# Attention and expert sums on one core: two banks for the weighted sums, other periods for the normalisation pieces, one rounding moved to VectorE

## The reference

```python
xn = _layernorm(x, axis=-1)
Q = einsum('bnd,hdk->bhnk', xn, proj_q); K = einsum('bmd,dk->bmk', xn, proj_k); V = einsum('bmd,dv->bmv', xn, proj_v)
weights = softmax(einsum('bhnk,bmk->bhnm', Q, K), axis=-1)
Y = einsum('bhnv,hdv->bnd', einsum('bhnm,bmv->bhnv', weights, V), proj_o)
mid = einsum('amh,ehn->aemn', xn, w1); ffn = einsum('aemn,enh->amh', mid, w2)
return x + Y + ffn
```

## Time and profile before

| what | us |
|---|---|
| median of 3 runs | 1715.02 |
| the runs | 1715.01, 1715.02, 1720.04 |
| the profiled execution | 1721.89 |
| its span | 1720.1 |
| PE busy | 1664.0 (97%) |
| POOL busy | 1334.9 (78%) |
| ACT busy | 1293.4 (75%) |
| DVE busy | 1280.9 (74%) |

### The profile page before, as it was taken

One profiled execution on the slowest core, in us unless ns is written; L12 is line 12 of the kernel. 1 busy time (PEld: TensorE's weight loads), 2 busy tenths in 40 slices (PEclk: granted clock), 3 DMA queues, 4 the chain that ended last, 5 costly groups with the idle time before them and its releaser, 6 DMA issues. The chain is left out here.

```text
span 1720.1 us, 46064 instructions
## 1 busy us (share of the span) xinstructions
PE 1664.0 (97%) x18808; PEld 1220.2 (71%) x18808; DVE 1280.9 (74%) x2754; ACT 1293.4 (75%) x1294; POOL 1334.9 (78%) x955
## 2 busy tenths in 40 slices
PE   6689999999999999999999999999999999999997
PEld 5567777777777777777777777777777777777774
DVE  4467777777777777777777777777777777777774
ACT  3467777777777777777777777777777777777774
POOL 0377887887887887888878878878878878788786
PEclk8899999999999999999999999999999999999999
DMA  7000000000000000000000000000000000000000
GB/s 223 1 2 2 2 2 8 8 2 2 2 13 3 2 2 2 14 2 2 2 8 8 2 2 2 8 8 2 2 2 8 8 2 2 2 14 2 2 2 13
DMA packets 16142, 16.70 MB, mean 10 GB/s; under 512 B 384, under 2 KB 12160, under 8 KB 15936
## 3 DMA queue, kind: packets, MB, share of 16 engines
q1 hardware_dynamic: 13856, 12.72, 2.5%
q10 hardware_dynamic: 2080, 1.05, 0.2%
HBM read 9.57 MB, written 4.19 MB: 8 GB/s over the span
## 5 line engine op out<-in xcount | busy, mean ns | idle before, releaser
L252 POOL TENSOR_TENSOR pr_lo<-pr,pr_hi 128x1024 f16<-128x1024 f32 x512 | 1087.6, 2135 | 338.8 <-ACT pr_hi L333 331.7
L326 ACT ACTIVATE pr<-s_ps,boost,scale 128x1024 f32<-128x1024 f32 x512 | 617.0, 1205 | 258.9 <-PE s_ps L457 240.9
L634 DVE TENSOR_REDUCE key_max<-s_ps 128x128 f16<-128x1024 f32 x512 | 625.9, 1223 | 0.5
L333 ACT ACTIVATE pr_hi<-pr 128x1024 f16<-128x1024 f32 x512 | 525.4, 1051 | 8.1
L455 PE MATMUL s_ps<-g_lo,xT 128*128 128x128 f16 x4096 | 516.1, 220 | 2.2 <-DVE g_lo L647 0.9
L457 PE MATMUL s_ps<-g_hi,xT 128*128 128x128 f16 x4096 | 515.6, 220 | 0.0
L455 PEld LDWEIGHTS s_ps<-g_lo,xT 128*128 128x128 f16 x4096 | 401.0, 98 | 42.3 <-DVE g_lo L647 10.1
L457 PEld LDWEIGHTS s_ps<-g_hi,xT 128*128 128x128 f16 x4096 | 402.5, 98 | 30.4 <-issue 0.6
L363 PE MATMUL t_ps<-pr_hi,xn_hi 128*128 128x512 f16 x1024 | 389.3, 380 | 21.0 <-POOL pr_lo L252 7.3
L365 PE MATMUL t_ps<-pr_hi,xn_lo 128*128 128x512 f16 x1024 | 389.2, 380 | 0.0
L364 PE MATMUL t_ps<-pr_lo,xn_hi 128*128 128x512 f16 x1024 | 389.2, 380 | 0.0
(11 more groups left out here) (108 smaller groups left out, 1548.8 us busy)
## 6 DMA issues: line engine op xcount, KB each, us to landing
out_dram<-xacc SPq DMA_DIRECT2D x16, 256.0 KB, 2.3
w_sb<-in_L_ffn_w_dram SPq DMA_DIRECT2D x1, 2048.0 KB, 12.9
xacc<-in_L_attn_x_dram SPq DMA_DIRECT2D x1, 640.0 KB, 7.9
pr<-in_L_attn_proj_q_dram ACTq DMA_DIRECT2D x1, 512.0 KB, 4.6
pr<-in_L_attn_proj_o_dram ACTq DMA_DIRECT2D x1, 512.0 KB, 6.8
wkv<-in_L_attn_proj_k_dram SPq DMA_DIRECT2D x1, 64.0 KB, 2.8
wkv<-in_L_attn_proj_v_dram SPq DMA_DIRECT2D x1, 64.0 KB, 4.4
w_sb<-in_L_ffn_w_dram SPq DMA_DIRECT2D x1, 0.5 KB, 19.1
```

Source lines behind the costliest of these rows:

```text
L252: pool.tensor_tensor(pr_lo[:, u % RING, :], pr32[:, u % PR, :], pr_hi[:, u % RING, :], ALU.subtract)\
L326: act.activation(pr32[:, u % PR, :], both_banks(u), ACT.Exp, bias=boost[:, 0:1], scale=scale[:, 0:1])\
L333: act.activation(pr_hi[:, u % RING, :], pr32[:, u % PR, :], ACT.Copy).then_inc(p_hi_ready, 1)
L634: dve.tensor_reduce(key_max[:, u % 2, :], both_banks(u).rearrange("p (t q) -> p q t", q=P), AX_X, ALU.max).then_inc(keys_max, 1)
```

## The change

- `t_ps` has two banks; block k sums into bank k mod 2 (`sum_bank`), and `turn_ps` is gone. The maxima are turned, and put into a row, in the bank that is idle; where n mod 4 = 2 they are turned in a half bank of the next unit's scores, whose second high pass therefore waits for `max_found`.
- Tile 0 of a block's sum moves from n mod 4 = 3 to the period before: its first product goes ahead of the turn of the maxima, the two others behind it. Every period then has two tiles. It waits for `p_lo_ready` 4k + 4 as before, for `t_lo_ready` k - 1 instead of k, and for a `bias_ready` that the low passes just before it wait for too.
- In n mod 4 = 3 the row of maxima is made right behind the second high pass, and `place_bias` stands ahead of `max_of_keys` as in the other periods.
- Normalisation pieces: `bn_stats` from n mod 8 = 2 to 0, `bn_aggr` from 3 to 1, epsilon from 6 to 3, `rstd` on GpSimd from 7 to 4, `normalise` from the next pair's 2 to the same pair's 7, `split_high` from 3 to 4, `xn_lo` on GpSimd from 4 to 5.
- The last unit's `pr_lo` and the last addition of head outputs go to VectorE.

```diff
-        t_ps = pb("t_ps", [P, BANK])
-        turn_ps = pb("turn_ps", [P, BANK])
+        t_ps = pb("t_ps", [P, 2 * BANK])
+        turn16 = t_ps[:, BANK:2 * BANK].bitcast(F16)
...
+        def sum_bank(k):
+            return t_ps[:, (k % 2) * BANK:(k % 2 + 1) * BANK]
+        def turn_bank(n):
+            return sum_bank(summing(n) + 1)
+        def maxima_turned(u):
+            if u % 4 == 2:
+                return bank(u + 1, 1)[:, 0:P // 2].bitcast(F16)
+            return turn_bank(u)[:, 0:P // 2].bitcast(F16)
...
-                if n % 8 == 7 and (tile := ln_tile(n // 8)) is not None:
+                if n % 8 == 4 and (tile := ln_tile(n // 8)) is not None:
                     pool.wait_ge(ln_var, tile - AHEAD + 2)
                     pool.tensor_tensor(rstd ...
-                if n % 8 == 4 and (tile := ln_tile(n // 8 - 1)) is not None:
+                if n % 8 == 5 and (tile := ln_tile(n // 8 - 1)) is not None:
                     pool.wait_ge(ln_hi, tile + 1)
                     pool.tensor_tensor(xn_lo ...
-                if 1 <= n <= UNITS:
+                if 1 <= n < UNITS:
                     p_low(n - 1)
...  (high_pass, half 1)
+                    if j == 3:
+                        pe.wait_ge(max_found, u)
...  (weigh)
-                if t == 0:
-                    pe.wait_ge(p_lo_ready, 4 * k + 4)
-                    if k == 0: pe.wait_ge(f_copied, 1)
-                    else: pe.wait_ge(t_lo_ready, k)
+                if first:
+                    if t == 0:
+                        pe.wait_ge(p_lo_ready, 4 * k + 4)
+                        if k >= 2:
+                            pe.wait_ge(t_lo_ready, k - 1)
+                        pe.wait_ge(bias_ready, min(4 * k + 6, UNITS))
+                        if k == 1:
+                            pe.wait_ge(f_copied, 1)
+                    pe.matmul(dst, xn_hi[:, tile, :], p_hi, start=t == 0, stop=False)
+                if rest:
+                    pe.matmul(dst, xn_hi[:, tile, :], p_lo, start=False, stop=False)
+                    done = pe.matmul(dst, xn_lo[:, tile, :], p_hi, start=False, stop=t == NT - 1)
...  (chunk)
+                k, t = summing(n), 2 * ((n + 1) % 4) + 1 + place
+                if t == NT:
+                    k, t = k + 1, 0
...  (PE's list)
+                at = n % 4
                 if n < UNITS: high_pass(n, 0)
-                if 1 <= n <= UNITS and not row_later: max_to_row(n - 1)
+                if 1 <= n <= UNITS and at != 3: max_to_row(n - 1)
                 if n < UNITS: high_pass(n, 1)
+                if 1 <= n <= UNITS and at == 3: max_to_row(n - 1)
                 chunk(n, 0)
-                if 1 <= n <= UNITS and row_later: max_to_row(n - 1)
-                chunk(n, 1)
                 small_products(n)
                 if 1 <= n <= UNITS: low_passes(n - 1)
+                if at == 2: chunk(n, 1, rest=False)
                 if n < UNITS: turn_keys_max(n)
-                chunk(n, 2)
+                chunk(n, 1, first=at != 2)
...  (VectorE's list)
+                if n == UNITS + 1:
+                    p_low_last()
+            dve.wait_ge(y_scaled, 2 * BLOCKS)
+            dve.wait_ge(ffn_added, TILES)
+            dve.wait_ge(y_added, 2 * BLOCKS - 4)
+            dve.tensor_tensor(xacc[:, last:last + 2, :], xacc[:, last:last + 2, :], y_tmp[:, 1, :, :], ALU.add)
```

More of the change, by code:

```diff
@@ L163, in both_banks, with summing, maxima_row @@
             return s_ps[:, at * BANK:(at + 2) * BANK]
-        def weighed(n):
-            m, q = divmod(n + 1, 4)
-            return m - 2, (((0,), (1,), (2,)), ((3,), (), (4,)), ((5,), (), (6,)), ((7,), (), ()))[q]
+        def summing(n):
+            return (n + 1) // 4 - 2
+        def sum_bank(k):
[6 more added lines that the diff above has]
+            return turn_bank(u)[:, 0:P // 2].bitcast(F16)
+        def maxima_row(u):
+            return turn_bank(u + 1)[:, 2 * P:3 * P]
         def ffn_tile(n):
@@ L193, in projected @@
         def projected(k):
-            return bank(4 * (k - 1) + 2, 1) if k >= 1 else t_ps[:, :]
+            return bank(4 * (k - 1) + 2, 1) if k >= 1 else sum_bank(0)
         def head_part(k, g):
@@ L281, in _ @@
                     head_adds += 1
-                if at == 0 and 0 <= k - 3 < BLOCKS:
+                if at == 0 and 0 <= k - 3 < BLOCKS - 1:
                     add_head(k - 3, 1, ffn_adds)
@@ L338, in t_high @@
                     act.wait_ge(y_ps, 2 * k)
-                act.activation(t_hi[:, :], t_ps[:, :], ACT.Copy).then_inc(t_hi_ready, 1)
+                act.activation(t_hi[:, :], sum_bank(k), ACT.Copy).then_inc(t_hi_ready, 1)
             g_high(0)
@@ L465, in turn_keys_max, with weigh @@
                     pe.wait_ge(bias_ready, u)
-                pe.transpose(turn16[:, 0:P], key_max[:, u % 2, :], ident16[:, :]).then_inc(turned, 1)
+                if u == 7:
+                    pe.wait_ge(f_copied, 1)
+                pe.transpose(maxima_turned(u), key_max[:, u % 2, :], ident16[:, :]).then_inc(turned, 1)
             def max_to_row(u):
                 pe.wait_ge(max_found, u + 1)
-                pe.matmul(turn_ps[:, 2 * P:3 * P], minus_max[:, u % 2, :], ident16[:, :], start=True, stop=True)\
+                if u % 4 == 2 and summing(u) >= 0:
+                    pe.wait_ge(t_lo_ready, summing(u) + 1)
+                pe.matmul(maxima_row(u), minus_max[:, u % 2, :], ident16[:, :], start=True, stop=True)\
                   .then_inc(rowed, 1)
-            def weigh(k, t):
-                if t == 0:
-                    pe.wait_ge(p_lo_ready, 4 * k + 4)
[L477 to L480, removed]
+            def weigh(k, t, first, rest):
                 tile = (batch_tile(k) + t) % KEEP
@@ L483, in weigh @@
                 p_hi, p_lo = pr_hi[:, at:at + 4, t * P:(t + 1) * P], pr_lo[:, at:at + 4, t * P:(t + 1) * P]
[L484 to L487, removed]
+                dst = sum_bank(k).rearrange("p (j c) -> p j c", j=4)
+                if first:
[5 more added lines that the diff above has]
+                        if k == 1:
+                            pe.wait_ge(f_copied, 1)
+                    pe.matmul(dst, xn_hi[:, tile, :], p_hi, start=t == 0, stop=False)
+                if rest:
+                    pe.matmul(dst, xn_hi[:, tile, :], p_lo, start=False, stop=False)
+                    done = pe.matmul(dst, xn_lo[:, tile, :], p_hi, start=False, stop=t == NT - 1)
+                    if t == NT - 1:
+                        done.then_inc(pv_done, 1)
             def fold_ffn(e):
@@ L493, in fold_ffn @@
                 for c in range(MC):
-                    last = pe.matmul(t_ps[:, 0:D], w1T[:, e, c * P:(c + 1) * P], w2_sb[:, e, c, :],
+                    last = pe.matmul(sum_bank(-1)[:, 0:D], w1T[:, e, c * P:(c + 1) * P], w2_sb[:, e, c, :],
                                      start=e == 0 and c == 0, stop=e == E - 1 and c == MC - 1)
@@ L497, in fold_ffn, with chunk @@
                     last.then_inc(f_ps, 1)
[L499 to L506, removed]
+            def chunk(n, place, first=True, rest=True):
+                k, t = summing(n), 2 * ((n + 1) % 4) + 1 + place
+                if t == NT:
+                    k, t = k + 1, 0
+                if k == -1 and rest:
+                    fold_ffn(t)
+                if 0 <= k < BLOCKS:
+                    weigh(k, t, first, rest)
             def head_out(k, g):
@@ L543, in _ @@
             for n in range(PERIODS):
-                row_later = n % 4 == 3
+                at = n % 4
                 if n < UNITS:
                     high_pass(n, 0)
-                if 1 <= n <= UNITS and not row_later:
+                if 1 <= n <= UNITS and at != 3:
                     max_to_row(n - 1)
@@ L550, in _ @@
                     high_pass(n, 1)
+                if 1 <= n <= UNITS and at == 3:
+                    max_to_row(n - 1)
                 chunk(n, 0)
-                if 1 <= n <= UNITS and row_later:
-                    max_to_row(n - 1)
-                chunk(n, 1)
                 small_products(n)
@@ L638, in find_max @@
                 dve.wait_ge(turned, u + 1)
-                dve.tensor_reduce(minus_max[:, u % 2, 0:1], turn16[:, 0:P], AX_X, ALU.max, negate=True)\
+                dve.tensor_reduce(minus_max[:, u % 2, 0:1], maxima_turned(u), AX_X, ALU.max, negate=True)\
                    .then_inc(max_found, 1)
@@ L646, in place_bias, with p_low_last @@
                     dve.wait_ge(g_lo_ready, k + 1)
-                dve.tensor_copy(g_lo[0:1, k % 2, j * P:(j + 1) * P], turn_ps[0:1, 2 * P:3 * P]).then_inc(bias_ready, 1)
+                dve.tensor_copy(g_lo[0:1, k % 2, j * P:(j + 1) * P], maxima_row(u)[0:1, :]).then_inc(bias_ready, 1)
+            def p_low_last():
+                u = UNITS - 1
+                dve.wait_ge(p_hi_ready, u + 1)
+                dve.tensor_tensor(pr_lo[:, u % RING, :], pr32[:, u % PR, :], pr_hi[:, u % RING, :], ALU.subtract)\
+                   .then_inc(p_lo_ready, 1)
             def t_low(k):
```

(27 more changed lines are left out.)

3 lines of the change are left out of this document (2 added, 1 removed).

## The result

The changed kernel takes 1777.29 us (median of 3 runs, 1765.29 to 1779.19) against 1715.02: ratio 1.033, 95% interval 1.027 to 1.039. It is slower, and the forecast of 1714.6 (range 1699 to 1733) was wrong. The profiled execution has a span of 1775.5 us, 55.4 more than before.

| stretch | before | after | difference |
|---|---|---|---|
| up to period 18 | 117.0 | 115.4 | -1.6 |
| periods 18 to 434, 52 pairs | 1333.3 | 1397.1 | +63.8 |
| periods 434 to 510 | 240.5 | 237.7 | -2.8 |
| from period 510 to the end | 29.2 | 25.3 | -3.9 |

The account below looks back on a forecast made before the run. TensorE, busy 1664.0 of 1720.1 us, was taken as the bound. Removed waits against a new GpSimd wait gave +1.6 us, the start +0.4, the end -2.4: -0.4 in sum, so 1714.6 us, range 1699 to 1733.

Parts of the forecast that it names:

- The two waits: TensorE's waits for t_lo (2 x 0.27 us a pair) and the bias row (0.19) both go: 44 us gross.
- What is late next: GpSimd's low parts make tile 0 wait 0.83 us once a pair, in n mod 8 = 6.
- the sum's claim: VectorE's moved normalisation pieces are not held by GpSimd, so the forecast sum has no cost for them.
- rival 2: VectorE's moved pieces, normalise above all, wait out GpSimd low parts: 1.4 us a pair, 1787 us; chance 0.09.
- the cast's way: VectorE's form that may use both ports and exclude GpSimd; normalise's 0.33 us against 0.20 was taken to speak against it.
- Rival 1: GpSimd's low parts don't bind TensorE, the gain arrives whole: pairs of 24.9 us, 1669 us; chance 0.15.
- Rival 3: TensorE waits for max_found ahead of the second high pass, n mod 4 = 3; if 0.2 us, 1730; chance 0.06.
- The end: Last low part and last addition on VectorE, each behind GpSimd's, and less half-pace running: -2.4 us in all.
- a term too small: At the end, a shorter TensorE standstill spares some of the half-pace products: -0.3 us, ends 0 and -1.6.
- The start: Block 0's tile 0 waits 0.5 to 1.2 us for GpSimd's low part, partly taken back: +0.4, ends -1 and +2.

Follow-up runs that it names:

- The fifth experiment, experiment 5: Changed kernel, normalise still in n mod 8 = 7, its output three gapped groups of 42, element 1 by its own instruction: 1718.63 us, ratio 1.0007.
- experiment 6: Changed kernel with normalise in n mod 8 = 6 and GpSimd's low part ahead of additions and rstd in n mod 4 = 0: 1672.19 us.

## Why the prediction was wrong

- **The two waits: right.** Both went; half pairs without a new wait take 12.48 us, as worked out (12.95 - 0.27 - 0.19 = 12.49). Together they were 0.73 us a pair, not 0.74.
- **What is late next: right, to 0.01 us.** In the changed kernel GpSimd's chain ends 15.30 us from the start of n mod 8 = 2 (15.31 forecast), and tile 0 starts 0.83 us late, once a pair. At the place shown the low part ends at 800.04 + 2.13 = 802.17 and the product starts at 802.22, the 0.05 of the earlier trace rows.
- **The step that failed is the sum's claim that VectorE's moved pieces cost nothing**, kept against rival 2 at 0.09. Rival 2 had the mechanism, the piece and a price (1.4 us a pair, 1787 us). Measured were 1.13 us a pair and 1777: the bias row is 1.54 late instead of 1.9, the low passes 0.75, and the rest 0.38 instead of 0.5. It even had what decides, on which side of a low part's start the piece is issued. The prediction set it aside for one reason: `normalise` takes 0.33 us and the cast 0.20, so it "seems not to run in the cast's way". That compared totals. The fifth experiment parts them: one element takes 0.266 us, 126 take 0.396, so each element costs (0.396 - 0.266) / 125 = 1.04 ns with the gaps, and about 0.266 are fixed. In the form of before, 0.332 - 0.266 is 0.066 us for 126 elements more, half as much each. So `normalise` did run in the cast's way; only its fixed part is larger (a cast of one element took 0.146 us in the same run). That its two per-row operands make the difference is likely, since epsilon's addition, one element without such an operand, takes 0.144 us, but no run isolates it. The rule of the Trainium skill that the prediction had cited was right, and the inference from the rows was wrong. The duration was also no evidence on the hold: no row of before had `normalise` beside a running GpSimd instruction.
- **The three pieces weren't alike.** Statistics and epsilon moved beside low parts too and kept 0.28 and 0.14 us. Only `normalise` was held.
- **Rival 1** had the right amount for a free kernel (pairs of 24.9 us); it took another order on GpSimd to get it. **Rival 3** didn't come: with no low part to wait for (experiment 6) it is in no pair, so a slack of about nothing was just enough.
- **The end: mechanism right, a term too small.** In the changed kernel:
```profile
1761.17 1.57 DVE L684 TENSOR_TENSOR pr_lo<-pr,pr_hi 128x1024 f16<-128x1024 f32 x1 [2.47 <-ACT pr_hi L350]
...
1762.79 0.39 PE L512 MATMUL t_ps<-pr_hi,xn_hi 128*128 128x512 f16 x1 [1.22 <-DVE pr_lo L684]
```
```profile
1759.52 2.13 POOL L268 TENSOR_TENSOR pr_lo<-pr,pr_hi 128x1024 f16<-128x1024 f32 x1
1761.61 1.71 POOL L280 TENSOR_TENSOR xacc<-xacc,y_tmp 128x256 f32<-128x256 f32 x1
```
  VectorE's low part waits for GpSimd's (until 1761.6), then holds GpSimd's addition, 1.71 us instead of 0.73: one behind the other, as put down. The product starts 12.60 us from period 510 instead of 14.28 (-1.7; -1.6 forecast). But TensorE stood 1.2 us instead of 3.25. Before, the granted clock behind that wait (1705.17 to 1708.30) is 0.50, that is 1.2 GHz, and the products of 512 columns start 0.43 us apart for 3.2 us; now it is 1.00 (2.4 GHz) from 1762.80 on, and they start 0.22 apart at once. That is -1.5, of which the prediction had counted 0.3. The last addition saves 0.6.
- **The start:** the wait at tile 0 of block 0 came, 1.2 us where 0.5 to 1.2 was forecast; `rstd` took 1.57 us there instead of 0.5 to 0.6. What gives it back could not be read: before the loop alone the traces differ by up to 2 us (it begins at 31.8 to 33.7).

What stays open: whether a `tensor_scalar` or cast of other lengths is held alike, whether it is the unequal lengths or the gaps as such that free it (experiment 5 has both), and how close behind a change of instructions one can come; only two places, 0.2 us apart, were tried.

## What to carry to other kernels

Before moving a VectorE instruction from SBUF to SBUF, look at what GpSimd does at the new time, and tell the instruction's form by its cost per element, not by its whole duration: in the trace of before this piece had never stood beside a running GpSimd instruction, and a row that lacks the collision is no evidence against it. When a wait is removed, sum from the rows which one comes next (here that was right to a few hundredths of a microsecond); then move that one too (here additions nobody waited for stood ahead of a low part that TensorE waited for). The same edit can be worth nothing before another change and 46 us behind it.

## What the runs showed of the hardware

- A held VectorE instruction ends 0.08 to 0.09 us behind the recorded end of the GpSimd instruction that held it, which is 0.12 to 0.15 behind the start of GpSimd's next one, and that one is not later for it (low parts keep their 2.09 us distance).
- The hold works both ways: GpSimd's addition of 0.73 us took 1.71 beside a VectorE subtraction with two inputs in SBUF.
- An output with gaps removed the hold of an fp32 `tensor_scalar` of 126 elements for 0.07 us of its own time, and 0.18 more until it starts, for the instruction that element 1 got. It removed that of the cast that reads the gaps too (0.27 us instead of 0.62).
- Not held beside a running GpSimd low part: the statistics (0.28 us), and one-element `tensor_scalar` instructions (0.14 and 0.27 us).
- After 1.2 us of standing (1.8 in experiment 6), TensorE's products went on 0.22 us apart per 512 columns, at a granted clock of 2.4 GHz; after 3.25 us they started 0.43 apart, at 1.2 GHz.
